# Recommendation tower on one core: ten one-hot tables, gathers in fours, a ring of three sample tiles and a new step order

## What is computed

```python
e = stack([tbl_f[ids[:, f]] for f in range(26)], axis=1)        # [2048, 26, 128]
sd = einsum('bfd,bd->bf', e, dense)
pairs = einsum('bfd,bgd->bfg', e, e)[:, iu, ju]                 # 325 of them
h = concatenate([dense, sd, pairs, dense], axis=1)
h = maximum(h @ W_top1 + b_top1, 0)                             # 512
h = maximum(h @ W_top2 + b_top2, 0)                             # 256
y = h @ W_top3                                                  # 1
```

## Time and profile before

| | |
|---|---|
| median of 3 runs | 402.63 us (401.68 to 403.55) |
| the profiled execution | 404.94 us |
| its span | 403.1 us |
| mean granted TensorE clock | 0.949 of full |
| instructions | 14210 |

### The profile page before, as it was taken

How to read it: one execution, slowest core, us unless ns; L and a number is a source line. 1 busy time by engine, 2 the same in 40 slices (tenths; PEclk the granted TensorE clock), 3 DMA queues, 4 the chain that set the end, 5 groups by cost and what they waited for, 6 DMA issues and landing times.

```text
span 403.1 us, 14210 instructions
## 1 busy us (share of the span) xinstructions
PE 337.3 (84%) x6216; PEld 301.7 (75%) x6216; DVE 234.1 (58%) x702; ACT 204.8 (51%) x289; POOL 277.5 (69%) x295
## 2 busy tenths in 40 slices
PE   0556889898989889897989899896998989898585
PEld 0545679797878769795979779683987979796384
DVE  0969968682776438680867457670587538640321
ACT  2372545566466534666465553754346654565132
POOL 6777777777777777777777777777777777773000
PEclk9998989999999989999998999998899999899559
DMA  6998233222323214223323325122141323111000
GB/s 166 246 260 261 77 84 96 79 76 83 98 81 78 76 54 110 68 80 81 96 80 79 81 57 121 55 81 78 55 122 54 99 62 81 55 52 36 3 2 1
DMA packets 19118, 35.33 MB, mean 88 GB/s; under 512 B 7168, under 2 KB 8712, under 8 KB 19056
## 3 DMA queue, kind: packets, MB, share of 16 engines
q0 software_dynamic: 9216, 18.89, 17.8%
q1 hardware_dynamic: 9824, 15.52, 13.9%
q10 hardware_dynamic: 16, 0.01, 0.0%
HBM read 34.39 MB, written 0.01 MB: 85 GB/s over the span
## 4 chain that ended last, share of the span: by engine, by line
PE 55%; POOL 12%; ACT 11%; DMA 9%; issue 8%; DVE 3%; SPq 1%; POOLq 0%
PE et_ps L565 23%; POOL rows L290 12%; PE m_ps L525 10%; PE g_ps L486 8%; ACT et L371 8%; PE m_ps L536 6%; PE et_ps L555 5%; DMA et<-tbl_in 5%; DMA rows<-tbl_in,idx 3%; ACT zt_hi L346 2%; PE m_ps L545 2%; DMA idb<-ids_one_hot 1%; DVE one_hot L406 1%; DVE zt_lo L449 1%; DVE z L442 1%
## 5 line engine op out<-in xcount | busy, mean ns | idle before, releaser
L290 POOL DMA_INDIRECT rows<-tbl_in,idx x288 | 276.7, 961 | 89.3 <-issue 84.8
L406 DVE TENSOR_SCALAR one_hot<-idb,first_row 125x256 fp32r<-125x256 int32 x512 | 159.6, 384 | 81.5 <-PE et_ps L565 78.5
L371 ACT COPY et<-et_ps 128x384 f32<-128x384 f32 (+1 forms) x128 | 123.4, 1031 | 97.8 <-PE et_ps L565 76.7
L565 PE MATMUL et_ps<-one_hot,table_hi 125*128 125x256 f32 x512 | 132.7, 297 | 22.2 <-DVE one_hot L406 18.8
L565 PE MATMUL et_ps<-one_hot,table_lo 125*128 125x256 f32 x512 | 127.1, 286 | 0.0
L565 PEld LDWEIGHTS et_ps<-one_hot,table_hi 125*128 125x128 f32 x512 | 100.1, 195 | 29.2 <-issue 20.4
L565 PEld LDWEIGHTS et_ps<-one_hot,table_lo 125*128 125x128 f32 x512 | 100.0, 195 | 0.0
L555 PE MATMUL et_ps<-ident,rows 128*128 128x128 f32 x288 | 51.1, 291 | 16.6 <-DMA rows<-tbl_in,idx 11.9
L486 PE MATMUL g_ps<-et 128*27 128x26 f32 x4096 | 54.0, 193 | 11.4 <-issue 9.2
L486 PEld LDWEIGHTS g_ps<-et 128*27 128x27 f32 x4096 | 45.3, 106 | 23.0 <-issue 15.9
L555 PEld LDWEIGHTS et_ps<-ident,rows 128*128 128x128 f32 x288 | 32.6, 145 | 22.3 <-issue 13.1
(11 more groups left out here) (46 smaller groups left out, 284.5 us busy)
## 6 DMA issues: line engine op xcount, KB each, us to landing
idb<-ids_one_hot SPq DMA_DIRECT2D x32, 256.0 KB
rows<-tbl_in,idx POOLq DMA_INDIRECT x288
et<-tbl_in SPq DMA_DIRECT2D x7, 448.0 KB
xt<-dense_t SPq DMA_DIRECT2D x8, 128.0 KB, 3.9
z<-w_z SPq DMA_DIRECT2D x2, 256.0 KB, 5.9
et<-w SPq DMA_DIRECT2D x1, 512.0 KB, 6.9
gram<-tbl_in SPq DMA_DIRECT2D x1, 448.0 KB
et<-tbl_in SPq DMA_DIRECT2D x7, 52.0 KB
```

Of the source, the lines that this page charges most:

```text
L290: nc.gpsimd.indirect_dma_start(out=rows[:, r, n, :], out_offset=None, in_=tables[GATHERED[k]], in_offset=bass.IndirectOffsetOnAxis(idx[par ...
L371: nc.scalar.copy(dst, src).then_inc(et_copied, 1)
L406: last = nc.vector.tensor_scalar(one_hot[n % 2][0:KP, k, :], idb[0:KP, n // 2 % ID_RING, n % 2, :], first_row[0:KP, 0:1], float(k), ALU.su ...
L565: last = nc.tensor.matmul(ps[:, n % 2 * CH:n % 2 * CH + CH], part[0:KP, n, k, :], one_hot[n % 2][0:KP, k, :], start=k == 0 and part is tab ...
```

## The change

- `ONE_HOT` gains tables 16 and 17: 10 one-hot tables, 16 gathered ones. A T step has four tables, a chunk has 8 T steps (four a tile), and the ring of rows has 6 slots of four.
- `et` becomes a ring of three tiles of 128 samples. G4 to G7 still come in the next phase, now waiting for their own tile's last T and the chunk's last pair.
- The products run half a chunk ahead: O0 to O4 of chunk c+1 stand at the end of the phase, O5 to O9 in the first half of the next. The order of the other steps changes too: T4, Z2 and G0 to G3 stand between Z1 and L0, and L0 follows G3.
- One-hot planes are a ring of 12. Each plane has its own wait and its own increments (`oh_ready`, `oh_used`). DVE has no B steps: at O of table n it builds table n+1, and this stands in its queue at that O's place.
- ACT copies a pair of products with two copies, one a tile (256 elements each), and the dense row with two.
- Staging has four places; SP loads a table when the low part of the one four before it is done. The ids of the fifth pair of tables (8 and 9) are loaded after all tables and after the last two weight transfers. The gathers' ids come in two transfers at the start. The weights are split at G3 of chunk 0, on DVE's queue between its build at O9 of chunk 0 and that at O0 of chunk 1.

```diff
-ONE_HOT = (1, 3, 4, 5, 6, 10, 12, 14)
+ONE_HOT = (1, 3, 4, 5, 6, 10, 12, 14, 16, 17)
...
+PHASE = [(step[0], int(step[1:])) for step in (
+    "T0 O5 G4 G5 T1 O6 G6 G7 O7 T2 A0 A1 T3 O8 A2 A3 O9 Z0 Z1 "
+    "T4 Z2 G0 G1 G2 G3 L0 O0 T5 O1 L1 T6 O2 T7 L2 O3 L3 O4").split()]
+def later(kind, n):
+    if kind == "O" and n < AHEAD:
+        return 1
+    return -1 if kind in "AZL" or kind == "G" and n >= G_STEPS // 2 else 0
+AHEAD = 5
-TR_TABLES = 3
+TR_TABLES = 4
-ROW_RING = 8
+OH_RING = 12
+ROW_RING = 6
+STAGES = 4
+PLAN = [(kind, p + later(kind, n), n) for p in range(-1, NCH + 1) for kind, n in PHASE
+        if 0 <= p + later(kind, n) < NCH]
...
+            # SP, start
             for n, f in enumerate(ONE_HOT):
-                if n >= 2:
-                    sp.wait_ge(table_in[n - 2], 32)
+                if n >= STAGES:
+                    sp.wait_ge(table_lo_done, n - STAGES + 1)
+                if n in (6, 8):
+                    load_ids(n // 2 - 1)
...
+            sp.wait_ge(table_lo_done, NO - 3)
             sp.dma_start(w2_raw...)
+            sp.wait_ge(table_lo_done, NO - 1)
+            sp.dma_start(w1_again, w1_dense[D:, :]).then_inc(w_in, 16)
+            sp.dma_start(w1_raw[KZ], w1_z[(KZ - 1) * 128:, :]).then_inc(w_in, 16)
+            for pair in range(4, NCH * PAIRS):
+                load_ids(pair)
...
+            # POOL
+            for i in range(NCH * TR_SLOTS):
+                wait(pool, t_done, i - ROW_RING + 1)
...
+            # ACT
+                if kind == "O" and n % 2 == 1:
+                    act.wait_ge(oh_used, (c * NO + n + 1) * KT)
+                    for t in range(TILES):
+                        last = nc.scalar.copy(et_fields(TILES * c + t, NG + n - 1, 2), src[:, t])
+                    last.then_inc(et_copied, 1)
...
+            # DVE
+            def build(unit):
+                pair, half = divmod(unit, 2)
+                if half == 0:
+                    dve.wait_ge(idb_in[pair % ID_RING], (pair // ID_RING + 1) * 16)
+                for k in range(KT):
+                    at = unit * KT + k
+                    wait(dve, oh_used, at - OH_RING + 1)
+                    nc.vector.tensor_scalar(one_hot[0:KP, at % OH_RING, :], idb[0:KP, pair % ID_RING, half, :],
+                                            first_row[0:KP, 0:1], float(k), ALU.subtract, ALU.is_equal)\
+                        .then_inc(oh_ready, 1)
+                if unit + 1 < NO:
+                    table_lo_part(unit + 1)
...
+            table_lo_part(0)
+            build(0)
+            for kind, c, n in PLAN:
+                if kind == "O" and c * NO + n + 1 < NCH * NO:
+                    build(c * NO + n + 1)
+                if kind == "G" and c == 0 and n == G_STEPS // 2 - 1:
+                    split_weights()
...
+            # PE
+                if kind in "TO" and (kind == "T" or n % 2 == 0) and SLOT[kind, c, n] >= 2:
+                    pe.wait_ge(et_copied, EMPTIED[STARTED[SLOT[kind, c, n] - 2]] + 1)
+                if kind == "O":
+                    for k in range(KT):
+                        at = (c * NO + n) * KT + k
+                        pe.wait_ge(oh_ready, at + 1)
+                        for part in (table_hi, table_lo):
+                            last = nc.tensor.matmul(ps[...], part[0:KP, n, k, :], one_hot[0:KP, at % OH_RING, :], ...)
+                        last.then_inc(oh_used, 1)
```

More of the change, by code:

```diff
@@ L81 @@
 W_LOADS = 16 * (KZ + 6)
+W_READY = 3 + 2 * (1 + KZ)
 def z_inputs():
@@ L194, in apart, with et_tile @@
             eng.sem_inc(waits_apart, 1)
[L196 to L212, removed]
+        def et_tile(tile):
+            return et[:, tile % ET_TILES * TILE_W:(tile % ET_TILES + 1) * TILE_W]
@@ L214, in _, with et_fields @@
+        def et_fields(tile, f, n):
+            return et_tile(tile).rearrange("d (b f) -> d f b", f=FW)[:, f:f + n, :]
         @block.sync
         def _(sp):
[L216 to L228, removed]
@@ new lines, in _ @@
+                if kind == "O" and c == 0 and n + STAGES < NO:
+                    table_hi_part(n + STAGES)
+                if kind == "G" and n % 2 == 1:
+                    bank = n // 2
+                    act.wait_ge(g_done, c * G_BANKS + bank + 1)
+                    if c == 0 and n == 1:
+                        act.wait_ge(table_lo_done, NO)
+                    dst = gram[:, :].rearrange("p (f g) -> p g f", f=F)[:, bank * G_GROUPS:(bank + 1) * G_GROUPS, :]
+                    src = g_ps[bank % 2][:, 0:G_GROUPS * F].rearrange("p (g f) -> p g f", f=F)
+                    nc.scalar.copy(dst, src).then_inc(g_copied, 1)
@@ new lines, in _ @@
+                if kind == "Z":
+                    act.wait_ge(a_done, c * A_USES + A_BANKS + n + 1)
+                    src = a_ps[(c * A_USES + A_BANKS + n) % 2][:, 0:CH].rearrange("z (q g) -> z q g", q=4)
+                    nc.scalar.copy(zt_parts[0][:, n, :].rearrange("z (g q) -> z q g", q=4), src)\
+                        .then_inc(zt_hi_done, 1)
+                if kind == "L" and n == 2:
+                    act.wait_ge(m_done, c * M_USES + 3)
+                    act.wait_ge(h1_split, c * 2 + 2)
+                    for m in range(2):
+                        last = nc.scalar.activation(h2[:, m, :], m_ps[0][:, m * CH:(m + 1) * CH], ACT.Relu,
+                                                    bias=b2s[:, m:m + 1])
+                    last.then_inc(m_free, 1)
@@ L374, in _ @@
+                if kind == "L" and n == 3:
+                    act.wait_ge(m_done, c * M_USES + 4)
+                    nc.scalar.copy(y, m_ps[1][0:1, 0:CH]).then_inc(m_free, 1)
+                    act.wait_ge(m_free, c * M_USES + 4 + 2)
+                    act.dma_start(out[:, c * CH:(c + 1) * CH], y).then_inc(y_out, 16)
             act.wait_ge(y_out, NCH * 16)
```

498 lines of the change are left out of this document (214 added, 284 removed).

## The result

The changed kernel takes 452.45 us (median of 4 runs, 451.57 to 453.28) against 403.09 for the kernel before in the same session: ratio 1.1224, 95% interval 1.1177 to 1.1271. It is slower, as forecast, but by twice as much: 427 was said, with 410 to 440, and the measured time lies above that range. The profiled execution took 453.28 us with a span of 451.5.

A forecast was written before the change was run, and what follows sets the result against it. PE's steps, with DVE's queue order stalling them, replace POOL as the bound: 74.0 + 6 x 47.4 + 37.4 + 31.9 = 427.7 us of span, 24.6 above 403.1, so a run of 427, range 410 to 440.

The forecast's parts named there:

- POOL's hold goes, PE's steps are the bound: Per chunk, POOL's gathers fall to 40.5 us while PE's bare steps sum to 41.1, so PE sets the pace.
- The stall at Z2 through DVE's queue: On PE, Z2 waits 2.1 us a phase for Z0's low part, queued on DVE behind table 0's planes.
- O1's planes behind L0's low part: DVE builds table 1's planes only after L0's low part, so O1 ends at 32.75 instead of 32.0.
- A handshake for each plane at no cost: On DVE, a wait and increment per plane keep the overlap: 2.5 us for a table's eight planes.
- The rival that priced it at 0.42: Per-plane handshakes cost DVE its overlap, 0.9 us more a table, giving 457; chance 0.06.
- The four G at 4.1 us: G0 to G3 in a row on PE, priced from the nearest row, a run of two G.
- The upper bound of 6.2: Upper price in us for four G in a row, from the last chunk's four; 12 us more in all.
- The pairs G4 G5 and G6 G7: Two-G runs early in PE's phase, each G priced singly at 0.72 us.
- my 47.4: One PE phase in us: 41.1 of steps, 1.2 for the four G, 5.1 of stalls.
- The start at 74.0: DVE sets the start; its tables, ids wait and weights put the first T0.1 at 74.0 us.
- The wait for ids: At the start, DVE waits about 6 us for the ids of tables 8 and 9, near 41 to 47.
- The end: From T0.7, 37.4 us to the end of L3, then a tail of 31.9 as before.

The follow-up runs named there:

- the last order: Changed kernel with no two G adjacent, ids early, Z's low parts first, start loads reordered and next-chunk planes behind Z2: 402.11 us, 0.9956 of the kernel before.

## Why the prediction was right in direction and wrong in size

*POOL's hold goes, PE's steps are the bound.* Right: POOL waited 56.8 us for T steps, and PE's phase, not POOL's, sets the pace. Its last gather ended at 392.4 where 368 was said, since T1.7 comes later, and 59 us before the end where 60 was said.

*The stall at Z2 through DVE's queue.* Right in mechanism: 2.1 was said, 1.0 to 1.8 measured (1.62 in the phase shown), with the very order of DVE's entries. That Z2 then started only 0.4 us later than said is part luck: the z copies began 0.95 us late, and eight planes took 2.2 to 2.3 us instead of 2.5. *O1's planes behind L0's low part.* Right in mechanism; they ran right up behind it, but L0 itself came late, so O1 ended at 35.75 of its phase where 32.75 was said.

*A handshake for each plane at no cost.* Right: 48 planes in a row took 14.78 us, 0.31 each, against 0.32 in the earlier trace rows. The rival that priced it at 0.42 gave 457 and stood nearest to the measured time, for a reason that isn't there.

*The four G at 4.1 us* is the step that failed first. The phase shown has 4.8, and the seven have 4.6 to 7.6, 5.4 on average, of which 1.7 are waits for instructions. The run that begins at 298.3 has two of them (1.63 and 1.95). The upper bound of 6.2, from the last chunk's run, was in my hands, and I weighed the shorter run more. The pairs G4 G5 and G6 G7, which I priced as two single steps of 0.72, took 1.9 and 1.75 from start to start, although the pair in the earlier trace rows with its 1.97 said so: 0.8 us a phase left out.

*The clock* is the term that wasn't there. All prices of single steps were taken from stretches at 2.4 GHz; only the last chunk's run of G had the low clock in it, from 374.2 on. In the changed kernel the granted clock falls from 2.4 to 1.2 GHz near the run of four G in five of seven phases: in four of them 0.4 to 4.1 us after its start, in one 0.6 us ahead of it and again in L0. In the one shown L0 takes 4.5 us instead of 2.9, and 3.0 to 4.8 over the seven, 3.9 on average. The clock's share can be read off the phases themselves: from L3 to L3 the two in which it stayed full have 48.7 and 49.0 us, the three complete ones in which it fell 50.1, 53.0 and 50.9. The phase shown is 2.7 us above my 47.4, and the terms are 0.7 for the G, 1.6 for L0 and 0.4 for a later Z2. Over the six phases the mean is 2.8: 1.4 for the G, 1.0 for L0, 0.4 for Z2. The Trainium skill, "TensorE: Matmul & The Clock Gate", section "HAM oscillation — how this bites in real kernels", ties the fall back to the lower clock to stretches in which PE stands idle between bursts. This case's runs agree only in part: the idle stretch at Z2 seems to matter (with at most 0.3 us of it, and no two G in a row, the clock fell in 2 of 21 phases), but with the same stretch and half the small matmuls the clock stayed full in six phases of seven. What in the run adds to it (the small size of its matmuls or the waits inside) no run here separates.

*The start at 74.0.* 80.2 was measured. The wait for ids was found and its length was right (5.87 against 6.0; taking it out gave 5.6), but I assumed that table loads stay ahead of DVE. They did not: DVE waited 1.00 us for ACT's high part of table 4 and 1.85 for ids, and 2.87 for PE, so the ninth low part ended at 46.0 and not at 41.4. After the weights PE then waited twice 1.26 us for copies.

*The end*: within 1 us in sum.

Of the 23.8 us that the sum lacked, 18 lie in the phases and their like at the end, most of it in the G runs and in L0 at the low clock, and 6 in the start. For the G price I had set a rule beside the rows: the Trainium skill, "Runtime: NRT & Kernel Launch", section "Instruction fetch mechanics", calls the edges of instruction blocks mostly hidden, which would make it 2.9. The runs disagree with that outcome: the waits are there, splitting the run or halving it removes nearly all of them, and the trace shows that they are instruction fetch, each at a block's edge and 1.28 to 1.54 us behind its packet. The trace agrees with the "mostly": the changed kernel has 51 packets, and 11 of them bring such a wait.

## What to carry to other kernels

When an order of work is written by hand, price each run of many short instructions as a run, by the longest such run in the trace, and look for what the clock does near it. Where a wait has no releaser, count the engine's instructions up to it and look at the instruction queue in the DMA part: the same 4096 small matmuls had idle time of 11.4 us before, 19.6 in the changed kernel and 9.8 in the last order. When one engine builds ahead for another, read its queue line by line: an engine busy 60% of the time held the bound one for 1 to 2 us a phase, because the urgent entry stood behind the one that could wait. Moving a bound from one engine to another at nearly the same pace wins only what the new bound leaves (45.3 to 43.9 us a phase here), and the part of the start that the old bound had covered comes out.

## What was not expected of the hardware

- PE can run out of instructions. A packet of 16 KB holds 256 of them (51 packets against 35 when 4096 instructions are left out), and all 97 waits inside G runs in twelve traces stand at the same place of such a block and end 1.19 to 1.64 us after a packet has landed. In the changed kernel four G in a row took 4.6 to 7.6 us, two in a row 1.74 to 1.94, and one alone in the last order 0.67 to 1.01 where no wait fell into it.
- The granted clock fell from 1.00 to 0.60 in five us in which PE was busy 3.96, behind an idle stretch of 1.62 us, and was back at 1.00 in the stretch from 210 on. In the profiled executions the mean clock of the ten-table kernels with the run of four was 0.923 to 0.942, with pairs 0.945 and 0.968, and with single groups 0.962 to 0.979; before the change it was 0.949.
- The eight-table version with T steps side by side had a clock of 0.877 and took 470 us with a fifth fewer one-hot matmuls than the changed kernel. Why its clock was so low is open.
